# Attention and a mixture of experts on one core: the shared part of the output goes through the buckets instead of straight to the output

## The chip, the cores and the metric

The kernel runs on one core of a Trainium2 chip. The metric is the device time of one execution in microseconds. Times before are given as the median of three runs and their spread.

## What is computed

For 128 sequences of 128 rows with 256 features, cut to what matters:

```python
x = x + differential_attention(ctx, layernorm(x))     # 16 heads, two softmaxes each
h = layernorm(x)
shared = silu(h @ ws_gate) * (h @ ws_up) @ ws_down
scores = sigmoid(h @ gate_w.T)                        # 16 experts, the best two
w = 2.5 * top2 / sum(top2)
routed = sum(w[k] * expert[k](h) for k in the two)    # silu(h@w_gate) * (h@w_up) @ w_down
out = x + shared + routed
```

## The kernel before

The program has two stages. Each engine has its own instruction stream, written out by hand, and they meet at semaphores.

**The steps.** 64 steps, one for two sequences, run as a software pipeline. Iteration `it` works on several steps at once: projections of it+3, stores of the split q and k parts of it+2, maxima of the scores of it+1, scores and attention of it, the second layer norm of it-1 (called d), and router and shared expert of it-2 (called r). On TensorE an iteration is 16 blocks (k = 0 to 15) of score matmuls with side work between them; ScalarE and VectorE follow the same k. Four iterations ahead of a loop and some behind it are written out; in the loop a body holds two iterations. SyncE's queue stores q and k parts to DRAM (`put_parts`), loads them again as stacks (`load_stacks(s, u, h)`, four parts a step), and puts the transposed maxima as two more rows into the q stack (`put_max(s, u)`, buffer mxT). TensorE needs the maxima of u = 0 at block 0 and those of u = 1 at block 8 of a step.

In iteration it, GpSimd does among others `norm_terms(d)` (the scale and shift, nb, of the second norm), `shared_add(r)` (base = shared expert + x, written into base_t), `numbers(r)` (token numbers in the rows), and `scatter(r, u, k)`: the normed row with its weights and numbers (rowt) goes by an indirect DMA to its place in the bucket of its first and of its second expert. ScalarE's `norm(d)` at k = 12 writes rowt and first waits, by

```python
wait_par(act, d_scat, SCAT, d.plus(-2))
```

until the scatters of step d-2 = it-3, which used the same buffer, have landed. SCAT is what one step adds to that semaphore. TensorE transposes rowt at k = 13 (L666). SyncE stores base_t to the output.

**The tiles.** The buckets are worked off in tiles of 128 rows, 144 tiles for the first experts and then 144 for the second. SyncE reads a tile's first row number from a table into a register (`load`, L333) and loads the rows (L456) ten tiles ahead; TensorE, ScalarE and VectorE compute the expert; VectorE multiplies by the weight. In the first pass GpSimd scatters the result into sums_dram, in the order of the second buckets (L1308). In the second pass SyncE also loads that part (L464), VectorE adds it, and GpSimd scatters the sum to the output's rows with an adding DMA (L1312). Rows that fill a bucket's last tile are written ahead by `pad_rows`: SyncE and ScalarE before the first tile, SyncE at tiles 16 to 31 for the second pass.

## Time and profile before

| | |
|---|---|
| median of 3 runs | 2264.52 us (2263.68 to 2272.43) |
| the profiled execution | 2255.66 us |
| its span, first to last instruction | 2253.9 us |
| its mean granted TensorE clock | 0.967 |
| TensorE busy | 2030.1 us |
| VectorE / ScalarE / GpSimd busy | 1452.9 / 1487.7 / 1468.8 us |

Busy times are sums over both stages, which have different limits. In the rows below PE is TensorE, PEld its weight loads, DVE VectorE, ACT ScalarE, POOL GpSimd, and SPq SyncE's queue. The numbers L... are lines of the kernel before.

### The profile page before, as it was taken

To read this page: it belongs to the slowest core of one execution; us is meant where nothing else is said; L and a number is where in the kernel's file an instruction comes from. 1 tells how busy PE (TensorE), PEld (TensorE's weight loads), DVE (VectorE), ACT (ScalarE), POOL (GpSimd) and SP (SyncE) were. 2 spreads that over 40 slices of the span, in tenths; PEclk is the share of its full clock that TensorE was granted. 3 is DMA by queue.
4 is the path that set the end of the run, shared out by engine and by line. 5 is a ranking of instruction groups with operands and counts; after the bars stand their busy time and mean duration, and the time that the engine had idled before them with its cause. 6 is when DMAs were issued, how large, how long until landed. Compare 5 with 4: busy or idle time off the path is not lost.

```text
span 2253.9 us, 75550 instructions
## 1 busy us (share of the span) xinstructions
PE 2030.1 (90%) x20273; PEld 1410.4 (63%) x20274; DVE 1452.9 (64%) x4326; ACT 1487.7 (66%) x3558; POOL 1468.8 (65%) x2116
## 2 busy tenths in 40 slices
PE   3888999999999999999999999999887999999896
PEld 2555666666666666666666666666555788776665
DVE  3566777777777777777777777777653344333333
ACT  2566777787877777778777877777653455444443
POOL 5346677676766766766676667667653565588777
PEclk8689999999999999999999999999987999999999
DMA  4676666666666766666666666666616655499996
GB/s 132 181 209 194 185 198 197 190 193 191 191 186 192 200 189 186 201 188 190 180 197 193 194 179 196 195 190 192 176 52 185 185 161 153 125 204 200 195 199 140
DMA packets 609905, 410.38 MB, mean 182 GB/s; under 512 B 436121, under 2 KB 563228, under 8 KB 609312
## 3 DMA queue, kind: packets, MB, share of 16 engines
q1 hardware_dynamic: 568736, 340.63, 54.8%
q0 software_dynamic: 39936, 67.69, 12.0%
q10 hardware_dynamic: 1152, 1.07, 0.1%
q8 instruction: 40, 0.66, 0.1%
q14 instruction: 41, 0.34, 0.1%
HBM read 215.71 MB, written 195.62 MB: 183 GB/s over the span
## 4 chain that ended last, share of the span: by engine, by line
SPq 35%; PE 30%; DMA 13%; issue 11%; DVE 6%; POOL 3%; ACT 1%; DVEq 0%; POOLq 0%; ACTq 0%
SPq L368 14%; DMA stacks<-mxT 8%; SPq L375 8%; PE mx_ps L490 5%; SPq L333 5%; PE mx_ps L740 4%; PE o_ps L523 3%; PE ms_ps L551 3%; DMA stack_dram<-kp 3%; SPq L456 3%; SPq L383 3%; PE ms_ps L572 2%; SPq L464 2%; DVE mx L935 2%; PE ms_ps L753 2%
## 5 line engine op out<-in xcount | busy, mean ns | idle before, releaser
L935 DVE TENSOR_REDUCE mx<-mx_ps 128x4 f32<-128x512 f32 x1024 | 695.3, 686 | 346.2 <-PE mx_ps L490 338.5
L797 ACT ACTIVATE prob<-st_ps 128x512 f32<-128x512 f32 x1024 | 606.2, 596 | 316.9 <-PE st_ps L483 300.0
L490 PE MATMUL mx_ps<-stacks 48*128 48x128 bf16 x4096 | 397.9, 221 | 112.8 <-DMA stacks<-mxT 92.0
L490 PEld LDWEIGHTS mx_ps<-stacks 48*128 48x128 bf16 x4096 | 232.9, 95 | 270.6 <-issue 148.8
L483 PE MATMUL st_ps<-stacks 50*128 50x128 bf16 x4096 | 396.4, 221 | 0.0
L523 PE MATMUL o_ps<-prob,v_sb 128*32 128x256 f32 x4096 | 331.6, 396 | 0.9 <-ACT oT L788 0.4
L740 PE MATMUL mx_ps<-w_gu_sb,prob 128*128 x1152 | 304.4, 387 | 0.0
L1255 POOL DMA_INDIRECT rows_dram<-rowt,posi x256 | 257.5, 1006 | 68.9 <-issue 64.0
L1121 DVE TENSOR_TENSOR prob<-prob,mx_ps 128x128 f32<-128x128 f32 x288 | 82.9, 288 | 323.4 <-ACT prob L881 321.5
L1312 POOL DMA_INDIRECT out<-stacks x144 | 225.0, 1562 | 61.5 <-issue 39.7
L483 PEld LDWEIGHTS st_ps<-stacks 50*128 50x128 bf16 x4096 | 230.6, 95 | 2.6 <-issue 1.5
L1308 POOL DMA_INDIRECT sums_dram<-stacks x144 | 141.7, 984 | 120.5 <-issue 83.1
L876 ACT ACTIVATE prob<-st_ps 128x256 f32<-128x256 f32 x288 | 110.7, 384 | 157.7 <-PE st_ps L732 152.5
L1188 POOL TENSOR_SCALAR ve<-mv 128x2 f32<-128x2 f32 x128 | 29.2, 228 | 282.3 <-DVE mv L966 277.5
L740 PEld LDWEIGHTS mx_ps<-w_gu_sb,prob 128*128 128x128 f32 x1152 | 198.0, 192 | 17.9
L881 ACT ACTIVATE prob<-mx_ps 128x128 f32<-128x128 f32 x288 | 80.0, 278 | 146.2 <-PE mx_ps L740 146.2
L753 PE MATMUL ms_ps<-w_dn_sb,v_sb 128*128 x576 | 172.6, 382 | 0.3 <-DVE stacks L1131 0.2
L534 PE MATMUL o_ps<-ident,oT 128*128 128x128 f32 x1024 | 167.6, 286 | 0.9 <-issue 0.6
L1242 POOL TENSOR_TENSOR x<-att,x_res 128x128 f32<-128x128 f32 x256 | 117.2, 458 | 58.9 <-POOL att L1235 55.2
L732 PE MATMUL st_ps<-ident,stacks 128*128 128x128 f32 x576 | 116.7, 285 | 40.3 <-DMA stacks<-rows_dram 38.0
L534 PEld LDWEIGHTS o_ps<-ident,oT 128*128 128x128 f32 x1024 | 107.3, 141 | 67.1 <-issue 53.1
L572 PE MATMUL ms_ps<-h2T,ws_gu_sb 128*128 128x256 f32 x512 | 146.5, 409 | 0.9 <-ACT h2T L858 0.9
(181 smaller groups left out, 4576.1 us busy)
## 6 DMA issues: line engine op xcount, KB each, us to landing
stacks<-stack_dram SPq DMA_DIRECT2D x512, 192.0 KB
stacks<-rows_dram SPq DMA_DIRECT2D x288, 130.0 KB, 2.6
stack_dram<-kp SPq DMA_DIRECT2D x128, 256.0 KB, 2.8
stack_dram<-qp SPq DMA_DIRECT2D x64, 384.0 KB
stacks<-sums_dram SPq DMA_DIRECT2D x144, 128.0 KB, 3.7
x_in<-in_x SPq DMA_DIRECT2D x64, 256.0 KB
c_in<-in_ctxT SPq DMA_DIRECT2D x64, 256.0 KB, 2.7
stack_dram<-qp SPq DMA_DIRECT2D x64, 256.0 KB
```

The source lines that it names most:

```text
L368: sp.dma_start(stack_dram[s.par(), n, r:r + m].rearrange("r h u d j t -> (d j) (r h u) t"), part[:, first:first + m, :].rearrange("p r (v ...
L483: return pe.matmul(st_ps[k % 2][:, i * P:(i + 1) * P], k_st[p][64 * h:64 * h + KROWS, u, j, :], q_st[p][64 * h:64 * h + KROWS, u, j, :], s ...
L490: return pe.matmul(mx_ps[k % 2][:, i * P:(i + 1) * P], q_st[p][64 * h:64 * h + ROWS, u, j, :], k_st[p][64 * h:64 * h + ROWS, u, j, :], sta ...
L523: mm = pe.matmul(OT[SLOT * g:SLOT * (g + 1), gg * SW:(gg + 1) * SW], v_sb[s.par()][:, (u * HEADS + 2 * c + i) * SLOT:(u * HEADS + 2 * c + ...
L534: mm = pe.transpose(out_ps, src, ident[:, :])
L572: mm = pe.matmul(M1[:, k * SW:(k + 1) * SW], ws_gu_sb[:, h, k * HID:(k + 1) * HID], h2T[:, h, :], start=(h == 0), stop=(h == DK - 1))
L740: mm = pe.matmul(gu_ps[t.off % 2][:, 0:2 * HID], rows_T[t.off % 4][:, h * P:(h + 1) * P], w_gu_sb[:, bass.ds(up, 1), h, :].rearrange("p e ...
L753: pe.matmul(eo_ps[t.off % 2][:, 0:D], hid_T[t.off % 4][:, :], w_dn_sb[:, bass.ds(down, 1), :].rearrange("p e n -> p (e n)"), start=True, s ...
L797: nc.scalar.activation(prob[k % 4][:, :], st_ps[k % 2][:, :], ACT.Exp, scale=float(HALF) ** -0.5).then_inc(a_exp, 1)
L935: v.tensor_reduce(mx[:, u, c * CHUNK:(c + 1) * CHUNK], mx_ps[k % 2][:, :].rearrange("p (c n) -> p c n", c=CHUNK), AX.X, ALU.max).then_inc( ...
L1255: g.indirect_dma_start(rows_dram[k][:, :], bass.IndirectOffsetOnAxis(ap=posi[p][:, u, k:k + 1], axis=0), rowt[p][:, u, :], None).then_inc( ...
L1312: g.indirect_dma_start(out_rows, bass.IndirectOffsetOnAxis(ap=row[:, C_TOK:C_TOK + 1], axis=0), sums, None, bounds_check=T - 1, oob_is_err ...
```

## The change

- The base (shared expert + x) is made by VectorE straight from PSUM at k = 10 (`shared_add`, semaphore v_base). ScalarE's copy of the bank and GpSimd's add go. SyncE's store of base_t to the output goes.
- GpSimd scatters the base of step it-3 in iteration it, in two halves around `norm_terms(d)`, to the places of the first buckets in a new tensor base_dram. These scatters count on d_scat as well, so SCAT is 6 x 16 instead of 4 x 16; ScalarE's line with that wait is as it was.
- In the first pass a tile loads its bases from base_dram as part, and VectorE adds to it. The second pass scatters to the output without adding. base_dram gets pads of its own, issued by GpSimd after the steps (d_padb).
- On SyncE `put_max(it, 1)` stands between the first and the other two q stores, and `put_max(b, 0)` between the two halves of `load_stacks(n2, 0, ...)`.
- A tile's first row is kept in a register from its row load to its part load (`first_row`), within one body of the loop: of 16 tiles in a body 10 are kept and 6 are loaded a second time.

```diff
-    out_g = out.rearrange("(g u) p d -> g p u d", u=2)
+    base_dram = nc.dram_tensor("base_dram", (N_FIRST, D), F32, kind="Internal").ap()
...
+        d_padb = sem("d_padb")
-        d_out = [sem(f"d_out{i}") for i in range(2)]
...
-        SCAT = 4 * 16
+        SCAT = 6 * 16
-        first, lo, hi, end = -4, 4, NS - 6, NS + 2
+        first, lo, hi, end = -4, 4, NS - 6, NS + 3
...
-            def put_parts(s, n, part, landed):
+            def put_parts(s, n, part, landed, runs):
 
                 for u in range(2):
                     for h in range(2):
                         wait(sp, d_stk[u][h], STK, s, -STK)
-                for r, first, m in (Q_RUNS, K_RUNS)[n]:
+                for r, first, m in runs:
...
-                    put_parts(n2, 0, qp, d_qw)
+                    put_parts(n2, 0, qp, d_qw, Q_RUNS[:1])
                 if it.is_in(0, NS):
                     put_max(it, 1)
                 if n2.is_in(0, NS):
+                    put_parts(n2, 0, qp, d_qw, Q_RUNS[1:])
                     wait(sp, g_ks, 1, n2, 1)
-                    put_parts(n2, 1, kp, d_kw)
+                    put_parts(n2, 1, kp, d_kw, K_RUNS)
...
-                    load_stacks(n2, 0, 0)
                 if b.is_in(0, NS):
                     put_max(b, 0)
+                if n2.is_in(0, NS):
+                    load_stacks(n2, 0, 0)
...
-                if r.is_in(0, NS):
-                    wait(sp, g_base, 1, r, 1)
-                    sp.dma_start(out_g[bass.ds(r.idx(), 1)].rearrange("g p u d -> (g p) u d"),
-                                 base_t[p][:, :, :]).then_inc(d_out[p], 16)
...
+            held = {}
+
+            def first_row(t):
+                if (t.k is None, t.off) not in held:
+                    held[t.k is None, t.off] = load(sp, row_tab[0:1, bass.ds(t.idx(), 1)], N_FIRST - P)
+                return held[t.k is None, t.off]
...
                     wait_par(sp, d_eo, 16, t.plus(-RING))
-                    r = load(sp, row_tab[0:1, bass.ds(t.idx(), 1)], N_FIRST - P)
+                    r = first_row(t)
                     sp.dma_start(tok[t.off % RING][:, :],
                                  rows_dram[t.off // NT][bass.ds(r, P), :]).then_inc(d_row[t.off % RING], 16)
                 t = j.plus(4)
-                if t.is_in(0, N_ALL) and t.off >= NT:
+                if t.is_in(0, N_ALL):
+                    if t.k is None and t.off == 0:
+                        sp.wait_ge(d_padb, 16 * E)
                     if t.k is None and t.off == NT:
                         for i in range(RING):
                             sp.wait_ge(d_eo[i], 16 * (NT // RING))
-                    r = load(sp, row_tab[0:1, bass.ds(t.idx(), 1)], N_FIRST - P)
+                    r = first_row(t)
                     sp.dma_start(part[t.off % RING][:, :],
-                                 sums_dram[bass.ds(r, P), :]).then_inc(d_part[t.off % RING], 16)
+                                 (base_dram, sums_dram)[t.off // NT][bass.ds(r, P), :]).then_inc(d_part[t.off % RING], 16)
 
...
-                    if k == 10 and do_r:
-                        wait(act, p_sd, 1, r, 1)
-                        wait(act, g_base, 1, r)
-                        nc.scalar.activation(sh_o[:, :, :], M0[:, :], ACT.Copy).then_inc(a_dn, 1)
...
+            def shared_add(s):
+                p = s.par()
+                wait(dve, p_sd, 1, s, 1)
+                wait(dve, g_x2, 4, s, 4)
+                wait_par(dve, d_scat, SCAT, s.plus(-2))
+                v.tensor_tensor(base_t[p][:, :, :], M0[:, :], x2[p][:, :, :], ALU.add).then_inc(v_base, 1)
...
+                    if k == 10 and do_r:
+                        shared_add(r)
...
+                    wait_par(dve, d_part, 16, t)
                     sums, weight = part[t.off % RING], tok[t.off % RING][:, C_W + t.off // NT:C_W + t.off // NT + 1]
-                    if t.off < NT:
-                        v.tensor_scalar(sums, eo_ps[t.off % 2][:, 0:D], weight, None, ALU.mult).then_inc(v_res, 1)
-                    else:
-                        wait_par(dve, d_part, 16, t, -16 * (NT // RING))
-                        v.scalar_tensor_tensor(sums, eo_ps[t.off % 2][:, 0:D], weight, sums, ALU.mult,
-                                               ALU.add).then_inc(v_res, 1)
+                    v.scalar_tensor_tensor(sums, eo_ps[t.off % 2][:, 0:D], weight, sums, ALU.mult,
+                                           ALU.add).then_inc(v_res, 1)
...
-            def shared_add(s):
-
-                wait(gp, a_dn, 1, s, 1)
-                wait(gp, a_n2, 2, s, 2)
-                wait(gp, g_x2, 4, s, 4)
-                wait_par(gp, d_out, 16, s.plus(-2))
-                g.tensor_tensor(base_t[s.par()][:, :, :], sh_o[:, :, :], x2[s.par()][:, :, :], ALU.add).then_inc(g_base, 1)
...
+                    wait_par(gp, d_scat, SCAT, s.plus(-2))
...
+            def scatter_base(s, u):
+
+                p = s.par()
+                g.indirect_dma_start(base_dram[:, :], bass.IndirectOffsetOnAxis(ap=posi[p][:, u, 0:1], axis=0),
+                                     base_t[p][:, u, :], None).then_inc(d_scat[p], 16)
...
+                if it.plus(-3).is_in(0, NS):
+                    wait(gp, v_base, 1, it.plus(-3), 1)
+                    scatter_base(it.plus(-3), 0)
                 if do_d:
                     norm_terms(d, mv2, nb2, ve2, v_s2, g_ve2, g_r2, g_nb2)
+                if it.plus(-3).is_in(0, NS):
+                    scatter_base(it.plus(-3), 1)
                 if do_r:
-                    shared_add(r)
...
-            for i in range(2):
-                gp.wait_ge(d_out[i], 16 * (NS // 2))
+            gp.wait_ge(v_pad, 1)
+            for e in range(E):
+                r = load(gp, pad_tab[0:1, e:e + 1], N_FIRST - P)
+                g.dma_start(base_dram[bass.ds(r, P), :], no_row[:, 0:D]).then_inc(d_padb, 16)
...
                             ap=row[:, C_TOK:C_TOK + 1], axis=0), sums, None,
-                            bounds_check=T - 1, oob_is_err=False, compute_op=ALU.add).then_inc(d_eo[t.off % RING], 16)
+                            bounds_check=T - 1, oob_is_err=False).then_inc(d_eo[t.off % RING], 16)
```

In the order of instructions, GpSimd's part of one iteration in the loop, from the maxima of it+1 to the residual, stood like this before (mv, ve and nb are the norm terms; line numbers of the kernel before):

```order
L1200 CAST mxp<-mx 128x2x16 [waits p_mT]
L1202 TENSOR_TENSOR mxp<-mx,mxp 128x2x16 [waits g_mxa]
...
L1188 TENSOR_SCALAR ve<-mv 128x2 [waits v_s2]
...
L1190 TENSOR_TENSOR mv<-ve,neghalf 128x2 [waits g_ve2]
L1193 TENSOR_SCALAR nb<-mv 128x1 [waits g_r2]
L1193 TENSOR_SCALAR nb<-mv 128x1
L1210 TENSOR_TENSOR base_t<-sh_o,x_1 128x512 [waits a_dn,a_n2,g_x2,d_out1]
L1250 TENSOR_SCALAR rowt<-rowt 128x2
...
L1235 TENSOR_TENSOR att<-o_sc 128x128 [waits v_cb,g_x2]
```

and stands like this now (line numbers of the changed kernel):

```order
L1208 CAST mxp<-mx 128x2x16 [waits p_mT]
L1210 TENSOR_TENSOR mxp<-mx,mxp 128x2x16 [waits g_mxa]
L1262 DMA base_dram<-base_t,posi 133120x256 [waits v_base]
...
L1196 TENSOR_SCALAR ve<-mv 128x2 [waits v_s2]
...
L1198 TENSOR_TENSOR mv<-ve,neghalf 128x2 [waits g_ve2]
L1201 TENSOR_SCALAR nb<-mv 128x1 [waits g_r2]
L1201 TENSOR_SCALAR nb<-mv 128x1
L1262 DMA base_dram<-base_t,posi 133120x256
L1251 TENSOR_SCALAR rowt<-rowt 128x2 [waits d_scat1]
...
L1235 TENSOR_TENSOR att<-o_sc 128x128 [waits v_cb,g_x2]
```

The add into base_t is gone from behind nb, and one scatter into base_dram stands ahead of the norm terms and one directly behind them.

SyncE's queue in one iteration, from the first q store to the k stores, before:

```order
L284 ISA [waits g_qs]
L368 DMA stack_dram<-qp 128x12x128 [waits d_stk00,d_stk01,d_stk10,d_stk11]
L368 DMA stack_dram<-qp 128x8x128
L368 DMA stack_dram<-qp 128x4x128
L284 ISA
L383 DMA stacks<-mxT 2x16x128 [waits a_mT]
L383 DMA stacks<-mxT 2x16x128
L368 DMA stack_dram<-kp 128x8x128 [waits g_ks,d_stk00,d_stk01,d_stk10,d_stk11]
L368 DMA stack_dram<-kp 128x8x128
```

and now:

```order
L283 ISA [waits g_qs]
L367 DMA stack_dram<-qp 128x12x128 [waits d_stk00,d_stk01,d_stk10,d_stk11]
L283 ISA
L382 DMA stacks<-mxT 2x16x128 [waits a_mT]
L382 DMA stacks<-mxT 2x16x128
L367 DMA stack_dram<-qp 128x8x128 [waits d_stk00,d_stk01,d_stk10,d_stk11]
L367 DMA stack_dram<-qp 128x4x128
L367 DMA stack_dram<-kp 128x8x128 [waits g_ks,d_stk00,d_stk01,d_stk10,d_stk11]
L367 DMA stack_dram<-kp 128x8x128
```

The two transfers of maxima moved ahead of two q stores, which have waits of their own now.

Further on in the same iteration, SyncE's loads for u = 0 and the maxima, before:

```order
L284 ISA [waits d_qw]
L375 DMA stacks<-stack_dram 48x1x2048 [waits d_kw]
L375 DMA stacks<-stack_dram 48x1x2048 x3
L284 REGISTER_ALU
L383 DMA stacks<-mxT 2x16x128 [waits a_mT]
L383 DMA stacks<-mxT 2x16x128
L284 ISA
L419 ISA [waits g_x2]
L419 DMA x_res<-in_x 128x2x256
```

and now:

```order
L283 ISA [waits d_qw]
L374 DMA stacks<-stack_dram 48x1x2048 [waits d_kw]
L374 DMA stacks<-stack_dram 48x1x2048
L283 REGISTER_ALU
L382 DMA stacks<-mxT 2x16x128 [waits a_mT]
L382 DMA stacks<-mxT 2x16x128
L374 DMA stacks<-stack_dram 48x1x2048 x2
L283 ISA
L420 ISA [waits g_x2]
L420 DMA x_res<-in_x 128x2x256
```

The maxima stand between two pairs of stack loads.

## Rows read from the trace of the kernel before

**Rows 1.** Page: busy tenths in 40 slices of 56.3 us
```profile
PE   3888999999999999999999999999887999999896
```

**Rows 2.** Windows: stretch, its length, busy of each engine (instructions), clock, DMA share, GB/s
```profile
200.00:1700.00 1500.00, 1389.85 (x16306) 920.34 (x16306) 1137.35 (x3473) 1143.11 (x2477) 1011.21 (x1659) 0.99 0.65 185
...
1764.00:1950.00 186.00, 185.57 (x1027) 156.37 (x1026) 80.63 (x228) 94.45 (x342) 111.09 (x114) 1.00 0.55 159
2000.00:2200.00 200.00, 181.40 (x914) 135.38 (x913) 72.09 (x203) 84.25 (x305) 159.57 (x103) 1.00 1.00 198
```

**Rows 3.** Waits, 200 to 1600 us: total, times, longest
```profile
POOL ve L1188 <- DVE mv L966: 214.1, 60, 6.1
...
PE mx_ps L490 <- DMA stacks<-mxT: 66.3, 77, 2.2
...
PEld mx_ps L490 <- DMA stacks<-mxT: 25.2, 25, 2.4
```

**Rows 4.** Groups by line, 200 to 1600 us: busy, mean ns, idle before
```profile
L935 DVE TENSOR_REDUCE mx<-mx_ps 128x4 f32<-128x512 f32 x900 | 611.1, 686 | 268.5 <-PE mx_ps L490 261.7 <-issue 5.4
...
L928 DVE TENSOR_TENSOR q_rest<-ms_ps,qp 128x512 f32<-128x512 f32 x57 | 38.9, 682 | 0.0
```

**Rows 5.** Timeline of one step: start, duration, instruction, idle before and its releaser
```profile
1030.52 0.23 PE L490 MATMUL mx_ps<-stacks 48*128 48x128 bf16 x1 [0.55 <-DMA stacks<-mxT]
...
1042.70 0.21 PE L490 MATMUL mx_ps<-stacks 48*128 48x128 bf16 x1 [0.63 <-DMA stacks<-mxT]
...
1049.03 0.50 POOL L1193 TENSOR_SCALAR nb<-mv 128x1 f32<-128x1 f32 x2 [0.21 <-POOL mv L1190]
1049.73 1.28 POOL L1210 TENSOR_TENSOR base_t<-sh_o,x 128x512 f32<-128x512 f32 x1 [0.20 <-issue]
...
1049.57 1.09 ACT L779 ACTIVATE rowt<-x,nb,mv 128x256 f32<-128x256 f32 x2
...
1051.23 0.60 PE L666 MATMUL ms_ps<-ident,rowt 128*128 128x128 f32 x4
...
1055.31 0.21 PE L490 MATMUL mx_ps<-stacks 48*128 48x128 bf16 x1 [0.76 <-DMA stacks<-mxT]
```

**Rows 6.** Chain that ended last, 1000 to 1055 us: start, us, what
```profile
1000.16 5.96 DMA stacks<-mxT
...
1040.65 1.91 DMA stacks<-mxT
```

**Rows 7.** GpSimd's scatters L1255 and L1308 by source: ns min/median/max, starts, landing
```profile
L1255 POOL DMA_INDIRECT rows_dram<-rowt,posi x256: 959/982/1236, 148.9 to 1698.7; - x128
...
L1308 POOL DMA_INDIRECT sums_dram<-stacks x144: 983/984/1001, 1723.1 to 1961.0; - x144
...
DMA to landing us min/median/max: 2.1/2.8/4.3
```

**Rows 8.** The adding scatter L1312 by source
```profile
L1312 POOL DMA_INDIRECT out<-stacks x144: 1559/1561/1599, 1967.0 to 2246.9; - x144
...
DMA to landing us min/median/max: 2.7/5.0/6.5
```

**Rows 9.** SyncE's row loads and register loads, 2000 to 2200 us, by source
```profile
L456 SPq DMA_DIRECT2D stacks<-rows_dram x102: 332/333/341, 2000.0 to 2199.7; - x102
...
L333 SPq TENSOR_LOAD <-row_tab x202: 261/272/741, 2000.5 to 2199.2; - x101
```

**Rows 10.** Windows of two early stretches
```profile
140.00:160.00 20.00, 18.40 (x217) 12.74 (x216) 12.36 (x34) 13.66 (x31) 13.29 (x21) 0.98 0.67 225
160.00:180.00 20.00, 16.33 (x171) 10.30 (x167) 13.30 (x44) 12.89 (x28) 9.12 (x15) 0.83 0.64 177
```

**Rows 11.** Timeline of SyncE's queue at the first tiles
```profile
1709.01 12.48 SPq L456 DMA_DIRECT2D stacks<-rows_dram  x16
1721.96 0.36 SPq L341 DMA_DIRECT2D rows_dram<-no_row  x1
1722.50 0.35 SPq L341 DMA_DIRECT2D sums_dram<-no_row  x1
```

More of the change, by code:

```diff
@@ L131, in program @@
         q_rest = sb("q_rest", [P, 512])
-        sh_o = sb("sh_o", [P, 2, D])
         nb1 = sb("nb1", [P, 2])
@@ L247, in program @@
         p_su, p_sd = sem("p_su"), sem("p_sd")
-        a_x, a_v, a_q, a_sh, a_dn = sem("a_x"), sem("a_v"), sem("a_q"), sem("a_sh"), sem("a_dn")
+        a_x, a_v, a_q, a_sh = sem("a_x"), sem("a_v"), sem("a_q"), sem("a_sh")
         a_k, a_n1, a_n2 = sem("a_k"), sem("a_n1"), sem("a_n2")
@@ L259, in program @@
                                                  sem("g_nb2"))
-        g_base, g_ve1, g_ve2 = sem("g_base"), sem("g_ve1"), sem("g_ve2")
+        v_base, g_ve1, g_ve2 = sem("v_base"), sem("g_ve1"), sem("g_ve2")
         passed = sem("passed")
@@ L386, in step @@
             def step(it):
-                b, n2, xs, r = it.plus(1), it.plus(2), it.plus(4), it.plus(-2)
+                b, n2, xs = it.plus(1), it.plus(2), it.plus(4)
                 p = it.par()
@@ L586, in clear @@
                 a, b, d, r = it.plus(3), it.plus(1), it.plus(-1), it.plus(-2)
-                users = {"M0": (((a_v, 1, b, 1),), ((a_e, 1, r, 1),), ((a_dn, 1, r, 1),), ((v_pf, 1, r, 1),),
+                users = {"M0": (((a_v, 1, b, 1),), ((a_e, 1, r, 1),), ((v_base, 1, r, 1),), ((v_pf, 1, r, 1),),
                                 ((a_k, 2, a, 2),)),
@@ L690, in _ @@
             pe.wait_ge(a_e, NS)
-            pe.wait_ge(a_dn, NS)
+            pe.wait_ge(v_base, NS)
             pe.wait_ge(a_k, 2 * NS)
@@ L1239, in residual @@
                     wait_par(gp, d_res, 16, s)
-                    wait(gp, g_base, 1, s.plus(-1))
+                    wait(gp, v_base, 1, s.plus(-1))
                     wait(gp, a_n2, 2, s.plus(-1))
```

## The prediction

> **What bounds the kernel now.** I read the page's slices first [rows 1]: TensorE is at nine tenths from slice 5 to 28 (to about 1640 us), drops around 1690, and is again nearly full to the end. So there are two stages: 64 attention steps, then 288 tiles in two passes of 144. The windows [rows 2] split them: TensorE is busy for 1389.85 of 1500 us in the steps; in the first pass it is full (185.57 of 186 us) with the DMA engines at 0.55; in the second pass TensorE idles for 18.6 of 200 us, the DMA engines stand at 1.00 and GpSimd is at 160 us.
>
> *The steps.* 900 score reductions in 1400 us, 16 to a step, give 56.25 steps, so one takes 24.9 us [rows 4]. The waits [rows 3] say what TensorE lacks: the maxima rows (stacks<-mxT), 66.3 us as a matmul wait and 25.2 us as a weight wait. GpSimd spends its spare time, 214.1 us, 3.8 a step, on one thing: the statistics of VectorE, before norm_terms. The step from 1030.52 to 1055.31 [rows 5] shows both waits for maxima (0.63 us ahead of block 8, 0.76 ahead of the next block 0), and one chain that matters below: GpSimd ends nb at 1049.53, ScalarE starts the norm of rowt at 1049.57, and TensorE transposes that rowt (L666) at 1051.23. The chain of waits [rows 6] has a maxima transfer that took 5.96 us to land, issued behind four stack loads, and one that took 1.91.
>
> *The passes.* GpSimd issued 114 scatters in 186 us and 103 in 200 us [rows 2], so a tile costs 1.63 us in the first pass, TensorE's own pace, and 1.94 in the second. There two things are full: GpSimd (1.56 us an adding scatter [rows 8] plus 0.3 idle) and SyncE's queue, which does a tile in 1.97 us (102 row loads in 200 us) with two register loads of 0.27 us median [rows 9] and no wait of its own.
>
> **The change part by part.**
>
> *1. Maxima issued earlier (steps).* put_max(it,1) moves ahead of two of the three q stores, put_max(b,0) ahead of two of the four stack loads. Both TensorE waits should go: 0.76 before block 0 is on the path and counts in full. Of the 0.63 before block 8 I count 0.4, since VectorE works without a gap from there to block 12. Gain about 1.2 us a step. On SyncE put_max(b,0) now comes before ScalarE has copied the maxima, and two stack loads, x_res and x_in are queued behind it; they are for the next step or later, and the out store's issue goes, so I cost that at nothing (the cover is the step itself; without it the two loads come 1 to 2 us late).
>
> *2. Base made by VectorE.* A 128x512 add that reads PSUM costs 0.68 us (the q_rest row of [rows 4]). It lands at k = 10, inside VectorE's packed stretch, and TensorE's prefix matmul now waits for it: +0.7 us on that stretch. GpSimd's 1.28 us add [rows 5] goes and two scatters come (2 x 1.28 with their gaps; 0.98 each in [rows 7]); its 3.8 us of idle takes them. The ScalarE copy of the bank goes too, hidden before and after.
>
> *3. The new wait.* This is the term that decides. scatter_base(it-3, 1) is issued by GpSimd right behind norm_terms(it-1). ScalarE's norm(it-1), at k = 12 of the same step, waits for d_scat of step it-3 at SCAT x n, and SCAT rises from 4 x 16 to 6 x 16. Before, those scatters were a whole iteration old. Now the norm cannot start until a scatter issued after its own terms has landed. Queued behind the norm on ScalarE are exp 13, the copies of q, exp 14 and h2T; TensorE waits for the norm at L666 and for the exps at blocks 14 to 0. I sum a step of [rows 5] anew, from block 0:
> - nb ends at 19.0, less 0.4 for the wait of block 8: 18.6
> - gap to the scatter on GpSimd: 0.3
> - scatter to landing: 3.2. The trace does not show this scatter; the nearest is L1308, of rows of the same size, at 2.1/2.8/4.3 us with the DMA engines at 0.55 [rows 2, 7]. Here they stand at 0.65 and SyncE's loads go at that moment, so I take a little over the median. Ends: 2.1 and 4.7 (its worst, and some load).
> - norm 1.1 and two hand-overs 0.2: the transposes start at 23.4 (21.0 would be possible without the new wait, base add included)
> - from the transposes to the next block 0: 1055.31 - 1051.23 = 4.08, less the 0.76 wait that goes: 3.3
>
> Period 26.7 us against 24.9: +1.8, in the 62 steps that have a step it-3: **+112 us** (ends: +43 at 2.1, +205 at 4.7). The gains of part 1 and the cost of part 2 are inside this sum.
>
> The Trainium skill, "DMA: Bandwidth & Descriptors", section "Anatomy of one DMA — SWDGE (gpsimd) path", fits a GpSimd DMA as about 2.0 us plus bytes over 436e3. For 128 KB that is an estimate of 2.3 us, near the minimum of the row, and the sum would come to 2343 us by it. The trace's median of 2.8 speaks for more.
>
> *4. TensorE's clock.* The new wait leaves TensorE idle for about 2.4 us in each step. Two early stretches [rows 10] show what idling does: with 18.40 of 20 us busy the granted clock was 0.98; with 16.33 busy it was 0.83, a third of the stretch at 1.2 GHz, and 171 matmuls were done, not 217. At 92 ns each these 46 are 4.2 us; 2.1 of them is more idling, so the low level itself cost about 2.1 us in 6.8, 0.3 us for each. I count 2 us of it in a step on the mean: 62 x 0.6 = **+37 us** (ends 0, and 93 with 5 us in each step).
>
> *5. The first pass.* Each tile now also loads its bases. A second DMA with its address costs SyncE 0.54 us (1722.50 - 1721.96 [rows 11]). For the first 26 tiles SyncE sets the pace (16 rows in 12.48 us, then the pads), so 26 x 0.52 = +13.5. In the loops one register load is left for a tile and 6 of 16 need a second: 1.97 - 10/16 x 0.36 = 1.75 us a tile, by rows taken with full DMA engines; with less traffic I take 1.71, against TensorE's 1.63: 96 tiles x 0.08 = +8. Ahead of this SyncE waits for d_padb: GpSimd starts its 16 pads of base_dram only after its last scatters (L1255 began last at 1698.7 [rows 7], two base scatters follow, so about 1701.5). At 1.28 us a pad they are out at 1722 and landed at 1724.7, while SyncE gets there at about 1709 + 7 x 0.8 = 1714.6: +10 (bounds: 0 if a plain DMA issues in SyncE's 0.33 us [rows 11], 15 if register loads add to each). Sum of the pass: +31.
>
> *6. The second pass.* The scatter no longer adds: 0.98 us for 1.56 on GpSimd [rows 7, 8], and one read of out less. GpSimd falls to 1.3 us a tile, SyncE to 1.72, TensorE stays at 1.63: (1.94 - 1.72) x 144 = -32. The tail (a backlog of scatters and 5.0 us of landing) shrinks by about 5. Sum -37. The two passes together: **-6 us**.
>
> Sum against the profiled execution's own 2255.7 us (2253.9 of span and 1.8 around it): 2255.7 + 112 + 37 - 6 = **2399 us**. That execution is 0.4% under the median of the runs shown, 2264.5.
>
> **The rivals.**
> *Faster, the wait is hidden.* If the landing comes before ScalarE would start anyway, the steps change by -1.2 + 0.7 = -0.5 each: 2255.7 - 31 - 6 = 2219 us, 2195 if the pads cost nothing. The point of decision: the landing must take under 24.9 - 23.5 = 1.4 us. For it speaks only that the profile gives no landing for a scatter in the steps; against it that none of 144 landed in under 2.1. Chance 0.09.
> *No change.* A landing of about 2.1 with the better pads and passes (-30) gives 2268, near the edge; VectorE's stretch costing more while the wait is hidden gives 2250. Chance 0.04.
> *Much slower.* The landing takes 4.7 and the clock falls in every step: 2255.7 + 205 + 93 - 6 = 2548. For it speaks that the early stretches lost the clock at 3.67 us of idle in 20 [rows 10]; against it, that the steps between 200 and 1700 us, with 110 us of idle in all, held 0.99 [rows 2]. Chance 0.1 of over 2500.
> *SyncE bounds both passes at 1.97 us.* If the kept registers save nothing, the first pass costs 0.34 x 96 = 33, 25 more than counted, and the second does not save its 32: 2399 + 57 = 2456. It is inside the range.
>
> **How the numbers follow.** The forecast (slower by 2285 to 2500) has 0.77, much slower 0.1, hidden wait 0.09, no change 0.04. The range 2285 to 2500 leaves a little over 0.2 outside, mostly at both far ends. A measurement of this kernel tells about 0.5% from no change: faster 0.09, same 0.04, slower 0.87.
>
> **What would show it.** In the profile after: ScalarE's rowt norm (now L785) idle for some 3 us before it, with the base_dram scatter as releaser; TensorE waiting at its transposes of rowt; no wait for stacks<-mxT; 16 reductions in 26 to 28 us; more slices with a lower granted clock. GpSimd's second-pass scatters at 0.98 us, DMA share near 0.8 in both passes, SyncE without waits. The prediction is wrong if the norm starts within 1 us of nb, or if TensorE finds other work in that time.

## The result and the profile after

| | before | after |
|---|---|---|
| median of the runs | 2264.1 us (2258.93 to 2272.43, 4 runs) | 2600.78 us (2586.56 to 2604.46, 4 runs) |
| ratio | 1 | 1.147, 95% interval [1.142, 1.153] |
| span of the profiled execution | 2253.9 us | 2601.1 us |
| granted TensorE clock, mean | 0.967 | 0.886 |

The change makes the kernel 15% slower; 2399 was forecast, with a range to 2500. The page after, busy tenths in 40 slices of 65 us, answers to [rows 1]; the two rows of the clock and the DMA engines stand with it:

```profile
PE   4888888888888878888888878888888579999997
...
PEclk7889888888888888888888888888896699999999
DMA  4676555555555555555555555555551477777775
```

TensorE has lost a tenth or two in every full slice of the attention steps, and the clock with it, while the tile slices at the right are as full as they were. The windows after (stretch, length, busy of PE, PEld, DVE, ACT and POOL, clock, DMA share, GB/s) answer to [rows 2]:

```profile
200.00:1600.00 1400.00, 1169.31 (x12515) 765.09 (x12512) 915.46 (x2676) 859.04 (x1860) 813.67 (x1313) 0.88 0.56 154
2130.00:2330.00 200.00, 193.15 (x1026) 154.54 (x1025) 81.45 (x228) 94.45 (x342) 111.58 (x114) 1.00 0.77 225
2360.00:2560.00 200.00, 196.84 (x1062) 160.50 (x1061) 84.17 (x236) 97.99 (x354) 116.03 (x118) 1.00 0.76 228
```

In the steps no engine is fuller than before, so something is waited for. The waits between 200 and 1600 us (total us, times, longest us), which answer to [rows 3], say what:

```profile
DVE mx L937 <- PE mx_ps L496: 439.0, 319, 7.2
...
POOL qp L1226 <- ACT qp L855: 224.4, 46, 5.4
ACT rowt L785 <- DMA base_dram<-base_t,posi: 210.6, 46, 7.2
PE ms_ps L672 <- ACT rowt L785: 171.5, 46, 6.5
...
PEld ms_ps L658 <- DVE base_t L983: 71.5, 45, 1.6
...
PE ms_ps L658 <- DVE base_t L983: 50.0, 45, 1.1
```

One row is new and starts the rest: once a step ScalarE's norm of rowt waits 4.6 us (210.6 / 46) for the landing of a base scatter. TensorE, VectorE and GpSimd wait behind it. The matmuls' wait for maxima rows is gone. The last two rows are a second new wait: TensorE's prefix matmul, once a step, for VectorE's base add. In the timeline of one step (start, duration, instruction, idle before it and its releaser), beside [rows 5]:

```profile
999.09 0.50 POOL L1201 TENSOR_SCALAR nb<-mv 128x1 f32<-128x1 f32 x2 [0.21 <-POOL mv L1198]
...
999.49 1.56 SPq L374 DMA_DIRECT2D stacks<-stack_dram  x2
...
999.80 1.09 POOL L1262 DMA_INDIRECT base_dram<-base_t,posi  x1 [0.21 <-issue]
...
1004.26 1.09 ACT L785 ACTIVATE rowt<-x,nb,mv 128x256 f32<-128x256 f32 x2 [4.11 <-DMA base_dram<-base_t,posi]
...
1005.41 1.11 PE L672 MATMUL ms_ps<-ident,rowt 128*128 128x128 f32 x4 [3.30 <-ACT rowt L785]
...
1007.16 1.17 POOL L1226 TENSOR_TENSOR qp<-q_rest,qp 128x512 bf16<-128x512 f32 x1 [4.45 <-ACT qp L855]
```

nb is done at 999.59, the scatter behind it starts at 999.80, and the norm at 1004.26: 4.67 us after nb and 4.46 after the scatter's start. Before, the norm began 0.04 us after nb. The four transposes then took 1.11 us where [rows 5] has 0.60. The windows of this step show why:

```profile
1000.00:1004.00 4.00, 1.95 (x23) 1.15 (x22) 3.09 (x15) 0.15 (x1) 2.01 (x4) 1.00 0.50 147
1005.00:1010.00 5.00, 4.59 (x34) 2.96 (x34) 1.38 (x2) 3.82 (x9) 2.38 (x3) 0.50 0.12 33
```

TensorE was busy for 1.95 of 4 us at the upper level of its clock; when the norm had come, it worked for 5 us at 0.50, which is 1.2 GHz.

Where the time went, from the first and last starts of the two scatters of the passes (144 each):

| | before | after |
|---|---|---|
| end of the steps, first scatter L1308 / L1321 | 1723.1 | 2078.4 |
| first pass | 237.9 | 265.1 |
| second pass, L1312 / L1325 | 279.9 | 243.1 |

Up to the first of these scatters the kernel lost 355 us, 336 of them between the first and the last block 0 of the steps. The first pass lost 27, the second gained 37.

### The profile page after: what moved, and what is told of

The parts are those of the page before. It is cut to its first block, busy times and chain, and to the rows that moved or that the text cites. A ratio compares the mean times of both kernels' runs of the same rounds, so it can differ in the third digit from the quotient of the medians.

```text
span 2601.1 us, 76078 instructions
## 1 busy us (share of the span) xinstructions
PE 2180.2 (84%) x20273; PEld 1498.0 (58%) x20274; DVE 1511.7 (58%) x4390; ACT 1458.2 (56%) x3494; POOL 1452.0 (56%) x2196
## 4 chain that ended last, share of the span: by engine, by line
PE 41%; issue 14%; SPq 13%; DMA 13%; DVE 10%; POOL 5%; ACT 2%; POOLq 1%; DVEq 0%; ACTq 0%
DMA base_dram<-base_t,posi 11%; PE mx_ps L496 8%; PE o_ps L529 7%; PE ms_ps L578 5%; SPq L332 4%; PE ms_ps L557 4%; SPq L470 4%; SPq L460 4%; PE o_ps L540 3%; PE ms_ps L672 3%; DVE mx L937 2%; PE ms_ps L558 2%; PE ms_ps L559 2%; PE ms_ps L586 2%; POOL mv L1198 2%
## 5 line engine op out<-in xcount | busy, mean ns | idle before, releaser
L496 PE MATMUL mx_ps<-stacks 48*128 48x128 bf16 x4096 | 424.8, 232 | 29.4 <-DMA stacks<-mxT 16.2
L489 PE MATMUL st_ps<-stacks 50*128 50x128 bf16 x4096 | 424.4, 232 | 0.0
L529 PE MATMUL o_ps<-prob,v_sb 128*32 128x256 f32 x4096 | 360.5, 427 | 0.4 <-ACT oT L794 0.4
L672 PE MATMUL ms_ps<-ident,rowt 128*128 128x128 f32 x256 | 68.0, 419 | 223.1 <-ACT rowt L785 223.1
L1226 POOL TENSOR_TENSOR qp<-q_rest,qp 128x512 bf16<-128x512 f32 x64 | 74.5, 1164 | 308.2 <-ACT qp L855 308.2
L785 ACT ACTIVATE rowt<-x,nb,mv 128x256 f32<-128x256 f32 x128 | 69.8, 592 | 276.7 <-DMA base_dram<-base_t,posi 275.5
L1321 POOL DMA_INDIRECT sums_dram<-stacks x144 | 141.7, 984 | 132.8 <-DVE stacks L1139 70.3
L1325 POOL DMA_INDIRECT out<-stacks x144 | 141.6, 983 | 107.2 <-issue 72.9
L540 PE MATMUL o_ps<-ident,oT 128*128 128x128 f32 x1024 | 184.6, 308 | 0.4 <-issue 0.2
L672 PEld LDWEIGHTS ms_ps<-ident,rowt 128*128 128x128 f32 x256 | 44.4, 211 | 236.8 <-issue 137.6
L1262 POOL DMA_INDIRECT base_dram<-base_t,posi x128 | 139.2, 1088 | 54.0 <-issue 54.0
```

The costliest lines, as they stand in the source:

```text
L489: return pe.matmul(st_ps[k % 2][:, i * P:(i + 1) * P], k_st[p][64 * h:64 * h + KROWS, u, j, :], q_st[p][64 * h:64 * h + KROWS, u, j, :], s ...
L496: return pe.matmul(mx_ps[k % 2][:, i * P:(i + 1) * P], q_st[p][64 * h:64 * h + ROWS, u, j, :], k_st[p][64 * h:64 * h + ROWS, u, j, :], sta ...
L529: mm = pe.matmul(OT[SLOT * g:SLOT * (g + 1), gg * SW:(gg + 1) * SW], v_sb[s.par()][:, (u * HEADS + 2 * c + i) * SLOT:(u * HEADS + 2 * c + ...
L540: mm = pe.transpose(out_ps, src, ident[:, :])
L672: mm = pe.transpose(M1[:, h * SW + u * P:h * SW + (u + 1) * P], rowt[d.par()][:, u, h * P:(h + 1) * P], ident[:, :])
L1321: g.indirect_dma_start(sums_dram[:, :], bass.IndirectOffsetOnAxis(ap=row[:, C_NEXT:C_NEXT + 1], axis=0), sums, None, bounds_check=N_FIRST ...
```

## Experiments

Eighteen runs, in sets that share a chip and its runs of the kernel before. A step is the median time between blocks 0 of 55 steps, in the profiled execution. "Own" is a semaphore of their own for the base scatters, "old adder" the ScalarE copy and GpSimd add of before, "early" both base scatters at the start of GpSimd's step.

| run | kernel | median, us | ratio to before | step, us |
|---|---|---|---|---|
| | before | 2264 | 1 | 24.9 |
| | after | 2601 | 1.147 | 30.8 |
| e1, g1 | own | 2332, 2345 | 1.010, 1.009 | 25.8, 26.0 |
| e2 | both scatters ahead of norm_terms | 2372 | 1.029 | 26.8 |
| e3 | filler matmuls | 2585 | 1.122 | 29.7 |
| e4 | old SyncE order | 2732 | 1.185 | 32.4 |
| f0 | after again | 2595 | 1.144 | 30.7 |
| f1 | before + SyncE order alone | 2221 | 0.978 | 24.2 |
| f2 | before + VectorE's add alone | 2284 | 1.007 | 25.5 |
| f3, h1 | own, old adder | 2204, 2212 | 0.970, 0.975 | 23.9, 23.9 |
| g2, h2 | own, old adder, registers loaded each time | 2284, 2260 | 0.984, 0.997 | 24.2, 24.0 |
| g3 | own, add 0.7 us earlier | 2348 | 1.009 | 26.0 |
| h3 | shared, old adder | 2608 | 1.151 | 30.8 |
| g4 | early, shared | 2643 | 1.137 | 31.2 |
| h4 | early, own, old adder | 2274 | 1.004 | 24.9 |
| i1 | early, own | 2640 | 1.138 | 31.2 |
| i2 | early, shared, old adder | 2482 | 1.070 | 28.2 |

The kernel before took 2306, 2324 and 2320 us (medians) in the sets of e, g and i, and 2267 and 2268 in those of f and h; ratios are always within a set. The same kernel's ratio still differs between sets by up to 0.013 (g2 and h2), and on the chips of e, g and i the tile stage took some 30 us longer (557 us in g1, 521 in h1), so a smaller difference between kernels of two sets shows nothing.

### First set: what the norm's wait is worth

e1 takes the norm's wait away and leaves everything else:

```
-  ...base_t[p][:, u, :], None).then_inc(d_scat[p], 16)     # SCAT = 6 * 16
+  ...base_t[p][:, u, :], None).then_inc(d_bsc[p], 16)      # SCAT = 4 * 16, BSC = 2 * 16
   (shared_add, positions and the end of the steps wait for d_bsc too; norm and numbers don't)
```

> The changed kernel, but the base scatters count on a semaphore of their own (two increments of 16 a step), so that ScalarE's norm waits only for the four row scatters that read rowt; VectorE waits for both before it writes the places anew, and for the base scatters before it writes base_t. Nothing is left out. Theory (the wait of the norm for the base scatter is the whole loss, with the clock that it costs): a step falls from 30.8 to between 24.0 and 24.9 us, the whole to 2255.7 - 6 for the passes - 0 to 50 for the steps, so 2200 to 2250 us, and the granted clock is back over 0.95. Rival A (the add on VectorE and the traffic of the scatters cost most of it): the step stays over 27 us, over 2370 us. Rival B (half and half): 2270 to 2370 us.

Ratio 1.010 [1.006, 1.015]. The norm starts 0.46 us after nb and the step falls from 30.8 to 25.8 us: 13.7 of the 14.7 per cent hang on this one semaphore. But the kernel isn't faster than before, which 2200 to 2250 us would have been. With 2332 us it lies in the range of rival B, even if some 40 us of that are this chip's, and the step is above the theory's 24.9. So the wait isn't the whole loss. The waits show what is left:

```profile
PEld ms_ps L660 <- DVE base_t L985: 83.9, 53, 1.6
PE ms_ps L660 <- DVE base_t L985: 58.5, 53, 1.2
```

The prefix matmul waits 1.1 us a step (58.5 / 53) for VectorE's add.

e2 keeps the semaphore and issues the second scatter ahead of the norm terms. It starts 16.8 us into the step where the kernel after has 19.2, and 3.7 us ahead of the end of nb, no longer 0.2 behind it:

```
                     scatter_base(it.plus(-3), 0)
+                    scatter_base(it.plus(-3), 1)
                 if do_d:
                     norm_terms(d, ...)
-                if it.plus(-3).is_in(0, NS):
-                    scatter_base(it.plus(-3), 1)
```

> The changed kernel with both base scatters ahead of the norm terms on GpSimd; nothing is left out and ScalarE's wait stays. The second scatter then starts some 1.3 us behind the first, 2 to 3 us earlier than now. Theory (what counts is the moment at which the last of these scatters lands): the wait of the norm shrinks from 4.5 us to about 1.5 to 2.5 us, a step to 27 to 28.5 us, the whole to 2360 to 2460 us. Rival (the landing does not follow the issue, since it is held up by SyncE's loads): the norm still starts 24 us behind block 0, and the time stays over 2560 us.

Ratio 1.029 [1.022, 1.037]: the theory, with a step of 26.8 us and a wait of 1.1 us instead of 4.6, even shorter than the 1.5 to 2.5 expected:

```profile
ACT rowt L785 <- DMA base_dram<-base_t,posi: 57.1, 51, 1.8
```

e3 keeps TensorE busy through the wait, with 14 matmuls of 512 columns on data that nothing reads:

```
+                    for _ in range(FILL):
+                        pe.matmul(M1[:, :], identb[:, :], idle_t[:, :], start=True, stop=True)
                     wait(pe, a_n2, 2, d, 2)
```

> The changed kernel with 14 additional matmuls of 512 columns (bf16, on constants, into the bank that the transposes overwrite) on TensorE ahead of its wait for the norm, about 3 us at full clock in each step, in a stretch in which it stood idle 3.3 to 3.6 us. Their result is not used. Theory (of the 5.9 us that a step is longer, about 2 are the low clock behind the idle stretch): the granted clock in the steps rises from 0.88 to over 0.95, the way from the transposes to the next block 0 falls from 5.4 to under 4 us, and the whole is 80 to 130 us shorter than the changed kernel, 2470 to 2520 us, although TensorE does more work. Rival (the clock only fills slack): no gain, or a loss of up to 60 us, 2580 to 2660 us.

Ratio 1.122 [1.117, 1.126], with a mean clock of 0.959. From the transposes to the next block 0 it is 3.4 us on the mean where the kernel after has 5.4, so the low clock cost 2.0 us a step there. Part of that was given back: nb ended at 20.1 us of the step (19.7 in e4 on the same chip, 19.0 in the kernel after on another), and the norm waited as before (214.5 us in 47). The net gain, 0.025 of 2306 or about 57 us, is under the 80 to 130 expected.

e4 puts SyncE's order back:

```
-                    put_parts(n2, 0, qp, d_qw, Q_RUNS[:1])
+                    put_parts(n2, 0, qp, d_qw, Q_RUNS)
 ...
                     load_stacks(n2, 0, 1)
+                    load_stacks(n2, 0, 0)
                 if b.is_in(0, NS):
                     put_max(b, 0)
```

> The changed kernel with SyncE's queue in the order of before: the maxima behind all three q stores and behind all four stack loads. Nothing is left out. With the loads ahead of the maxima, two of them no longer run beside the second base scatter. Theory (the scatter lands late, 4.5 us behind its issue where I had counted 3.2, because those two stack loads now share the DMA engines with it): the landing comes 0.8 to 1.5 us sooner, and as the maxima have time enough in a 30 us step, the whole falls by 50 to 90 us, to 2510 to 2550 us. Rival (the landing does not depend on them): the same landing, and the time is that of the changed kernel within 30 us or longer, as the maxima come later.

Ratio 1.185 [1.180, 1.191]. I expected a gain, since fewer loads would go beside the second scatter; it was the other way. The norm starts 5.9 us after nb instead of 5.05. In the DMA records of one step the second scatter's first data moves 2.6 us after its start and its last at 5.7. Ahead of it four stack loads had been issued, and the data of x_res, issued 0.5 us behind it, moves first as well. In the kernel after, 30 of this scatter's 48 packets are done 2.2 us after its start and the last at 4.0.

The semaphore tells the same over 50 steps. The second scatter is counted in full 4.7 us after its start in the kernel after (4.3 to 5.4) and 5.5 in e4 (median). In the step shown above ten of its 16 increments come at 2.4 to 2.5 us and six at 3.7 to 4.4. A stack load of the same step also leaves six late increments, so the late six are probably on engines that both use, but the records don't name engines. The first scatter of a step, whose two stack loads are issued 0.5 and 1.4 us behind it and move their data mostly after it, is counted in full at 2.5 us (2.5 to 2.6) in the kernel after. So the landing is long because of SyncE's traffic at that moment.

### Second set: the parts alone

```
f1: the two SyncE edits of the diff on the kernel before, nothing else
f2: shared_add on VectorE at k == 10 on the kernel before; SyncE still stores out from base_t
f3: e1 with ScalarE's copy at k == 10 and GpSimd's shared_add ahead of numbers(r)
```

> The kernel before with one part of the change alone: the order of SyncE's transfers in a step (query parts stored in two pieces with the second maxima between, the second stack load behind the first maxima). The output store, the adder and the tile stage are those of before. Theory A, the order is worth what the matmul of block 8 waited for maxima in before (66 us in 77 waits between 200 and 1600 us): that wait goes and the ratio to before is 0.97 to 0.985. Theory B, that wait covers work that is late anyway (VectorE and ScalarE are still behind when block 8 begins): the wait goes, others grow by as much, ratio 0.995 to 1.005.

Ratio 0.978 [0.975, 0.982]: theory A by its number. The step falls by 0.7 us, and the wait for maxima from 66.3 (and 25.2 as a weight wait, [rows 3]) to this:

```profile
PE mx_ps L492 <- DMA stacks<-mxT: 44.5, 48, 2.3
...
PEld mx_ps L492 <- DMA stacks<-mxT: 0.7, 2, 0.4
```

By its mechanism it is not theory A. The gaps of more than 0.15 us ahead of block 0 (44.0 us in 48 steps before) are the ones that went, and those ahead of block 8, which the theory named, grew from 24.7 us in 32 steps to 50.3 in 55.

> The kernel before with one part of the change alone: VectorE adds the shared expert's rows to the residual straight from PSUM, ScalarE's copy and GpSimd's add are gone, the output store on SyncE stays and no scatter of base rows is made. Theory A, the prefix matmul waits 1.1 to 1.6 us a step for VectorE's add (there were 53 such waits in the kernel with its own semaphore) and this delays the step: ratio 1.01 to 1.03. Theory B, ScalarE and GpSimd gain 0.4 to 1.5 us of free time a step and the wait is made up: ratio 0.98 to 1.00.

Ratio 1.007 [1.004, 1.010], 15 us or 0.25 us a step. Between the theories, nearer to A. The trace has a step 0.6 us longer than the kernel before's on another chip; the runs on one chip are the better figure.

> The changed kernel with a semaphore of their own for the base scatters, as in the run before, and in addition with the adder of before (ScalarE copies the shared expert's rows out of PSUM, GpSimd adds them to the residual). Theory A, VectorE's add is what was left of the loss: the prefix matmul's waits for it go and the ratio to before falls from 1.010 to 0.97 to 0.99. Theory B, the rest lies in GpSimd's two further scatters a step or in the tile stage, and GpSimd, with its add back, is later still: ratio 1.01 to 1.03, with longer waits of ScalarE for GpSimd's norm bias or of GpSimd for nothing.

Ratio 0.970 [0.967, 0.974]: theory A. This kernel beats both. nb and the norm are where they were before (19.0 and 19.05 us into the step), and TensorE is fuller in the steps than in the first row of [rows 2]:

```profile
200.00:1600.00 1400.00, 1345.90 (x15974) 892.97 (x15966) 1129.41 (x3349) 1115.14 (x2423) 1094.99 (x1719) 1.00 0.68 195
```

> The changed kernel as it stands, for a trace on the same chip as the others of this set. Theory: 1.14 to 1.155 of before on this chip as well, with 4 to 5 us a step between the norm bias and the norm.

Ratio 1.144 [1.138, 1.149], as expected.

### Third set: adder, registers, and the place of the scatters

> The kernel with a semaphore of its own for the base scatters and VectorE's adder, a second time. Its ratio to before was 1.010 in a set in which the kernel before took 2306 us, 40 us more than in the other sets. The parts measured one by one since then (transfer order 0.978, VectorE's add 1.007, and 0.992 for the scatters and the tile stage, out of 0.970 by 0.978) multiply to 0.977. Theory A, the first set's chip was the reason and the parts add: ratio 0.97 to 0.985. Theory B, VectorE's add costs more together with the scatters than alone: ratio 1.00 to 1.015, norm bias 1 us later in the step than 19.0 us again.

Ratio 1.009 [1.006, 1.012]: theory B. VectorE's adder costs more beside the scatters than alone: the step is 26.0 us where the old adder of g2, on the same chip, has 24.2. That difference is one of medians; from the first block 0 to the last, 63 steps, it is 1638 against 1552 us, so 86 us, 1.4 a step, or 3.7%, against 0.7% in f2. Of the 1.8 us between the medians 1.1 lie ahead of nb, which comes at 20.4 us of the step and not at 19.3, and 0.6 between nb and the transposes.

```
g2:  r = first_row(t)   becomes   r = load(sp, row_tab[0:1, bass.ds(t.idx(), 1)], N_FIRST - P), twice
g3:  shared_add(r) directly behind stats(d, ...) at k == 9, no longer at k == 10
g4:  scatter_base(it-3, 0) and (it-3, 1) first in GpSimd's step, ahead of key_rest
```

> The kernel with its own semaphore and the old adder (0.970), but SyncE loads a tile's row number into a register at each of its transfers, as before, instead of keeping it: 288 register loads more. Theory A, SyncE waits for nothing it could issue earlier in the tile stage (its transfers are 10 and 4 tiles ahead), so the ratio stays at 0.968 to 0.973 and the stage at 520 us. Theory B, the loads delay the transfers of parts: the stage is 5 to 20 us longer, ratio 0.973 to 0.98.

Ratio 0.984 [0.978, 0.990]. f3, its twin, ran on another chip, so the set h repeats the pair.

> The kernel with its own semaphore, VectorE's add moved ahead of its maximum of block 10 (0.7 us earlier). Theory A, the prefix matmul's wait for the add is what VectorE's adder costs: the wait shrinks from 1.1 to 1.6 us to 0.4 to 0.9 us a step and the time is 0.3 to 0.7 us a step under that of the kernel with the add in its old place (ratio lower by 0.008 to 0.018). Theory B, the adder's cost lies in VectorE's and PSUM's time and not in that wait: the two kernels are within 0.004 of one another.

Ratio 1.009 [1.006, 1.013], the same as g1, though the wait shrank:

```profile
PEld ms_ps L660 <- DVE base_t L985: 55.1, 53, 1.1
...
PE ms_ps L660 <- DVE base_t L985: 29.8, 52, 0.7
```

29 us less of the matmuls' wait gave nothing back: theory B. What the adder costs beside the scatters is not that wait alone. Why nb comes 1.1 us later was not separated.

> The changed kernel with the shared semaphore kept, and both base scatters moved to the start of GpSimd's step, ahead of the key split, some 8 to 10 us before the norm bias. Theory A, the loss is the lateness of the landing against the norm and not the shared semaphore as such: both land before the norm bias is ready, the norm waits for none, and the ratio falls from 1.147 to that of the kernel with its own semaphore (0.98 to 1.01). Theory B, 2.2 us more of GpSimd at the start of its step delays the key split, whose parts SyncE stores and loads again for the matmuls: ratio 1.02 to 1.06, with PE waiting for stacks.

Ratio 1.137 [1.130, 1.144]. Both theories missed. The norm waits for no scatter any more (it starts 0.46 us after nb), but nb itself comes at 25.5 us of the step and not at 19.0. In the windows of one step all of TensorE, VectorE and ScalarE stand still at once, while GpSimd goes on:

```profile
1022.00:1024.00 2.00, 1.67 (x21) 1.06 (x20) 1.81 (x6) 0.79 (x3) 1.70 (x2) 1.00 0.93 307
1024.00:1026.00 2.00, 0.38 (x2) 0.00 (x0) 0.00 (x0) 0.00 (x0) 1.67 (x3) 1.00 0.56 188
1026.00:1028.00 2.00, 0.34 (x3) 0.34 (x4) 0.69 (x1) 1.08 (x2) 1.67 (x4) 1.00 0.70 194
```

### Fourth and fifth sets: the twins

```
h1: f3 again      h2: g2 again      h3: f3 with the scatters on d_scat, SCAT = 6 * 16
h4: f3 with g4's place      i1: g4 with its own semaphore      i2: h4 on d_scat
```

> The kernel with a semaphore of its own for the base scatters and the old adder, a second time, beside the one that loads its registers each time. It gave 0.970 [0.967, 0.974] in a set where before took 2267 us. Theory A, the ratio carries over between chips: 0.966 to 0.978 here. Theory B, on the chips where before takes 2306 to 2324 us this kernel gains less, as the one with VectorE's adder did (1.009 on two such): 0.978 to 0.99 if this set falls on such a chip.

> The same kernel with SyncE's row numbers loaded at each transfer; it gave 0.984 in another set, 0.014 above the kept registers, but not on the same chip. Theory A, the difference was the chip's: within 0.004 of the kernel with kept registers here. Theory B, the 288 loads cost 10 to 30 us: 0.005 to 0.014 above it.

Ratios 0.975 [0.968, 0.982] and 0.997 [0.994, 1.001] on one chip: theory A for the repeat, theory B of the registers, and more than it named, 48 us. It lies in the tile stage, from the first scatter to the end of the span: 521.3 against 572.8 us (ahead of it h2's profiled execution was 12 us shorter). The traces have 378 and 576 register loads, so 198 were saved and not 288. The windows of the second pass, h1 first, then h2:

```profile
2000.00:2200.00 200.00, 196.78 (x1048) 158.25 (x1046) 83.56 (x235) 96.22 (x349) 115.02 (x117) 1.00 0.76 224
```

```profile
2000.00:2200.00 200.00, 187.76 (x951) 141.06 (x950) 75.33 (x212) 87.50 (x317) 103.85 (x107) 1.00 0.70 204
```

GpSimd issues 117 scatters in the one and 107 in the other: 1.71 and 1.87 us a tile. SyncE's register loads in the same stretch, h1 and then h2 (ns min/median/max):

```profile
L334 SPq TENSOR_LOAD <-row_tab x153: 261/270/594, 2000.9 to 2190.8; - x153
```

```profile
L334 SPq TENSOR_LOAD <-row_tab x209: 262/270/533, 2000.0 to 2199.7; - x105
```

1.31 and 1.95 loads a tile; 0.64 x 0.27 is 0.17 us, and a tile differs by 0.16. So without the kept registers SyncE's queue sets the pace of both passes, and with them it is level with TensorE.

> The changed kernel with the old adder and nothing else altered: the base scatters count on the shared semaphore again. Beside the best kernel of this set it differs by the semaphore alone. Theory A, the semaphore is the whole loss and the adder plays no part in it: ratio 1.12 to 1.15, norm 4 to 5 us after its bias. Theory B, with GpSimd's add between, the second scatter is issued at another moment than the stack loads and the wait shrinks: ratio 1.02 to 1.08.

Ratio 1.151 [1.142, 1.159], theory A. Beside h1, its twin on the same chip, the semaphore alone is worth 0.175, or 396 us, of which 379 lie between the first and the last block 0: the step is 30.8 against 23.9 us. Its waits have the row of the kernel after once more:

```profile
ACT rowt L786 <- DMA base_dram<-base_t,posi: 246.7, 45, 8.2
```

> The best kernel (semaphore of their own, old adder) with both base scatters at the start of GpSimd's step, ahead of the key split. With the shared semaphore and VectorE's adder this place gave 1.137 although the norm waited for no scatter. Theory A, that loss came from GpSimd's order (the key split 3.4 us later): it shows here as well, ratio 1.08 to 1.14. Theory B, it came from the shared semaphore, by a wait other than the norm's: ratio 0.97 to 1.00 here.

Ratio 1.004 [1.000, 1.008]. At the upper end of theory B, but 3% above h1 all the same; not the 8 to 14 of theory A. The common stall of g4 is not there.

> Both base scatters at the start of GpSimd's step, VectorE's adder, and a semaphore of their own. Its twin with the shared semaphore gave 1.137, the kernel with the old adder and an own semaphore at this place 1.004. Theory A, the shared semaphore is what cost there, through a wait that is not the norm's: ratio 1.03 to 1.05 here (1.004 and the 4 per cent by which VectorE's adder stood above the old one). Theory B, it was VectorE's adder together with the early scatters: ratio 1.10 to 1.14.

> Both base scatters at the start of GpSimd's step, the old adder, and the shared semaphore. Theory A, the shared semaphore cost at this place too: ratio 1.08 to 1.14. Theory B, the adder did: ratio 1.00 to 1.01, since the norm finds both scatters landed.

Ratios 1.138 [1.128, 1.147] and 1.070 [1.060, 1.079]: theory B for i1, neither for i2. With the early place the semaphore makes no difference under VectorE's adder (g4 and i1 agree), so g4's loss is not a second wait on it; with the old adder it makes 6.6 points (i2 against h4). The waits of i1 and then i2 show the same stall, in all 44 steps of the one and in half of the other's (the first row of each is TensorE behind ScalarE's copy of the values; VectorE waits at the same time, for what the trace calls "remote"):

```profile
PE ms_ps L588 <- ACT v_sb L818: 136.1, 44, 3.4
...
DVE mx L939 <- remote: 113.9, 44, 3.9
```

```profile
PE ms_ps L587 <- ACT v_sb L817: 61.1, 23, 3.6
```

Some 3 us are lost in a step whenever it strikes. TensorE waits for ScalarE; ScalarE and VectorE wait for something that the trace marks "remote", which names no releaser. VectorE's is the semaphore of the score matmuls of block 3. It rises 3.9 us after they start in all of 55 steps of g4 and 4.0 in 53 of i1, 3.2 in 27 of i2, where 0.4 us is usual (block 0 and 1 of g4's step), and in none of the kernels before, after, h1 and h4. Why it is late stays open, and so does what either adder or semaphore has to do with it.

## Why the prediction was wrong

The mechanism was right in its place, and its size was not. 2601 us is above even the 2548 of the rival "much slower". Point by point:

- **The new wait (3).** Shown: own semaphore against shared, 0.975 to 1.151 with all else equal. The step that failed is the term "scatter to landing: 3.2". The semaphore has the landing 4.7 us after the scatter's start (median of 50 steps; 4.3 to 5.4), and from nb to the norm it is 5.05 us (24.07 less 19.02), where gap and landing were counted as 3.5. I took the landing of a scatter of the first pass; this one goes beside two 48-partition stack loads and is counted in full only when the last six of its 16 increments come. The 4.7 given as the far end was the median.
- **"less 0.4 for the wait of block 8: 18.6".** Measured 19.0: the wait went and nb didn't move. In f1, where nothing else changed, the wait ahead of block 8 even grew and the gain came from block 0, whose 0.76 was counted rightly. The transposes start at 25.3 us, not 23.4.
- **The clock (4).** "I count 2 us of it in a step on the mean" was the other failure. The low level was granted for 358 us in 47 stretches between 200 and 1640 us (before: 20.5 in 5), so for 7.6 us in each of 47 steps, mostly in pieces of 6.8. The price of 0.3 us for each held: from the transposes to the next block 0 it took 5.4 us, forecast 3.3 and 0.6 for the clock, and e3 shows that 2.0 of the 5.4 are the clock. Two early stretches with idle time scattered in them were the wrong model for a wait in one piece.
- **The sum.** 0.4 + 1.55 + 1.5 = 3.45 us a step more than forecast, x 62 = 214; the time was off by 202. Both ends had been written down, 4.7 us for the landing and 93 us for the clock, and were given 0.1 for coming together. They are not independent: a longer wait is also a longer idle stretch. "The cost of part 2" is not inside the sum as it says, since none of its terms has the 0.7; that none was due (h3 against after) was luck.
- **Maxima (1).** The waits went. Alone the order gives 0.7 us a step (f1), forecast 1.2, and takes away only the wait of block 0.
- **VectorE's add (2).** "+0.7 us on that stretch" is an upper bound for the part alone (f2: 0.25 by the runs of one chip, 0.6 by the traces of two), and too little beside the scatters once the norm no longer hides it: 1.4 on the mean (g1 against g2). Under the shared semaphore it costs nothing (h3 against after). This decides the rival in which the wait is hidden: its 2219 us, 0.98 of before, counted VectorE's add at 0.7, and with the wait gone that kernel measures 1.01; only with the old adder is it 0.970 and 0.975. Its point of decision, 1.4 us of landing, is where a step would be as long as before; the -0.5 a step of its own sum asks for 0.9.
- **Passes (5, 6).** +27 and -37, forecast +31 and -37. The near hit is in part luck: the pads delayed SyncE by 2.1 us, not 10, since a plain DMA by GpSimd took 0.54 us, and the pass itself was slower than the 21 counted for it. A kept register was counted at 0.36 us, which no row gives; it saves 0.27 (h1 against h2). SyncE had no cover to spare, as counted: the rival "SyncE bounds both passes", +57 us without the kept registers, is what h2 measures, 51.5.

## What to carry to other kernels

When a transfer is added to a semaphore that others wait on, look for each waiter and ask when its youngest transfer is now issued. Here a wait that had always been an iteration old became one for a DMA issued after the waiter's own input. A semaphore of its own turned 1.15 into 1.01 with the change's adder, and into 0.975 with the old one. Take the landing of such a transfer from one that goes beside the same traffic, and count the clock together with the idle time that causes it. And change an edit of several parts one part at a time: of those here the transfer order and the kept registers gain, VectorE's add and the shared semaphore lose. The bases that go through the buckets make the first pass 24 us longer, and with the scatter that doesn't add and the kept registers the second 35 shorter (h1 against before, on two chips).

## What the runs showed of the hardware

- The same 128 KB scatter landed in 2.5 us when it had the engines nearly to itself, in 4.7 beside two stack loads, and in 5.5 behind four of them (medians). The Trainium skill's fit for a GpSimd DMA ("DMA: Bandwidth & Descriptors", section "Anatomy of one DMA — SWDGE (gpsimd) path") gives an estimate of 2.3 us, which is near the first of the three.
- One wait of 3.7 us on TensorE in a step of 31 (171.5 / 46) was followed by 1.2 GHz for 7.6 us a step on the mean; its matmuls there took 1.11 us for 0.60. With the wait filled by matmuls (e3) the mean clock was 0.959 where it had been 0.886. In the kernels with neither this wait nor the stall of g4 it was 0.955 to 0.976.
- A register load on SyncE took 0.27 us, as much as four fifths of a DMA's issue (0.33 us). 99 of them in each pass were worth 29 us in the first and 22 in the second when its queue set the pace (h2 against h1).
